# Attention and GRU in one kernel: the softmax's reciprocals through DRAM instead of TensorE, and another sequence of SyncE's transfers

## The chip, the cores and the metric

The kernel runs on one core of a Trainium2 chip. The metric is the device time in microseconds (us), the median of the runs shown. Engines: TensorE (PE, with its weight loads as PEld), VectorE (DVE), ScalarE (ACT), GpSimd (POOL), SyncE (SP), which here only issues DMA transfers, and the 16 DMA engines that carry them out.

## The reference, cut to what matters

`x` is 16 batches x 256 rows x 512, `cond` 16 x 512, all float32. An attention layer with 16 heads of 32 is followed by a GRU over the 256 rows.

```
xn = rms_norm(x, g_norm) * (1 + scale) + shift      # scale, shift = cond @ W_emb + b_emb
q, k, v = split(xn @ W_qkv); q, k = rms_norm(q, g_q), rms_norm(k, g_k)      # by head
attn = softmax(q k^T * 32 ** -0.5); o = attn v
x = x + o + o @ W_out
x = x + GRU(x, h0 = cond)                           # 256 steps, one after the other
```

## The kernel before

**Stages.** After a start of some 70 us comes the attention for the 16 batches, up to about 660 us, and then the 256 steps of the GRU up to the end, which the change leaves alone apart from how its weights `wih` are loaded.

**Passes.** The attention is done in 64 passes (`NP`), four for each batch b. Pass p = 4 b + w (w from 0 to 3) takes one half of the rows (i = 0 for w 0 and 1, i = 1 for w 2 and 3) and 8 of the 16 heads, in two units e = 0, 1 of four heads j. In a pass TensorE does: `scores` of the next pass (L612), `turn_p` of the two units, which transposes the exponentials P (L631), `turn_recips` (L654), two pieces of other work that the table `slots(p)` lists, and `times_v` (L646), which gives O for the pass with the dimension of a head on the partitions: partition 32 j + d, free (e, row). The pieces are mostly projections for the next batch n = b + 1 (`project`, 12 products, L552) and the output projection (`out_proj`, 12 products, L667). All projections and output projections use PSUM bank 6 in turn, so each waits until the one before was read out of it (`bank6_empty`). In w = 0 the pieces are `project(n, 0, 1)` and `project(n, 1, 1)`.

**Reciprocals.** The sums of the exponentials (`rsum`) stand with the row on the partition, but O needs their reciprocals with the row along the free dimension. So DVE takes the reciprocal at the end of pass p - 1 for pass p (`recips(p)`, L1041), spreads the 8 numbers of a row over 256 (`rB`, L1045), TensorE transposes them in pass p (L654) into bank 7, ACT copies them to `rTs` (`keep_recips`, L1305), and DVE multiplies O by them at the start of pass p + 1 (`scale(p)`, L947). In that same pass TensorE's `turn_p` waits for `scale` before its fifth transpose (semaphore `o`), since O and P transposed share a bank.

**The x of the next but one batch.** In w = 2 DVE turns the block-wise x of batch b + 1 out of the buffer `xb` (`turn_x`, L858, which counts `x_blocks_turned` up). SP may then load the x of the following batch into `xb` (`load_x`, L308): 16 DMAs of 32 KB, since each moves 32 partitions of one column block. In w = 0 ACT squares all of it (`square_blocks`, L1212, output `sqx`), which waits for all 16. It is the first thing that ACT does in a pass with w = 0; behind it stand, in this order, the copy of P transposed (`PT`, L1311), `keep_recips`, four exponentials with their sums (L1296), the copy of the projection out of bank 6 (`keep_raw`, L1251), its squares (L1270), `PT` again, four exponentials, `scale_q` (L1282), the second `keep_raw` and its squares. In w = 1 DVE sums these last squares and POOL raises them to the power -1/2 (`rsqrt`, L1486), then POOL scales `xb` for the next `turn_x`.

**Order.** All of it is written by hand: each engine runs its own list, and semaphores couple them. SP's list for a batch b is `load_x(b + 2)`, `store_q`, `load_q` (the q rows go through DRAM to be blocked), then the transfers of the output rows of batch b - 1 (`store_x1`, `load_residual`, `store_blocks`), `store_k`, `load_k`, and the output rows again. A wait of SP holds up all that stands behind it.

Of the kernel before, what the change touches and what calls it, by code (L numbers as in the profile page):

```python
# [5 lines left out]
F32 = mybir.dt.float32  # L6
# [6 lines left out]
NB = 16  # L13
T = 256
D = 512
# [13 lines left out]


# [20 lines left out]
for _p in range(NP):  # L51
    PASS += [("recips", _p)] + [_x for _slot in slots(_p) for _x in _slot if _x]
# [32 lines left out]
def cond_resid_kernel(nc, x, cond, W_emb, b_emb, g_norm, W_qkv, g_q, g_k, W_out, W_ih, W_hh, b_ih, b_hh, out):  # L85
    gscr = nc.dram_tensor("gscr", [NT, 128, 4, 3, 128], F32, kind="Internal").ap()
    xscr = nc.dram_tensor("xscr", [T, NB, D], F32, kind="Internal").ap()

# [5 lines left out]
    with ExitStack() as ctx:  # L94
# [30 lines left out]
        rinv = sb("rinv", [128, 8])  # L125
        rB = sb("rB", [128, 2, 128])
        rTs = sb("rTs", [128, 2, 256])
# [137 lines left out]
        s_wl = sem("wo_low_parts")  # L265
        s_gd = [sem("first_gates0"), sem("first_gates1")]
# [25 lines left out]
        def _(sp):  # L292
# [4 lines left out]
            def load_x(b):  # L297
# [7 lines left out]
                for a in range(4):  # L305
# [105 lines left out]
            for b in range(NB):  # L411
                if b + 2 < NB:
                    load_x(b + 2)
                if b:
                    store_q(b)
                    load_q(b)
                if b == NB - 1:

                    sp.wait_ge(s_qkv, 6 * b + 4)
                    for j in range(4):  # L420
                        for k in range(2):
                            load_whh(j, k)
# [4 lines left out]
                else:  # L427
                    load_residual(0, 0)
                    load_residual(0, 1)
# [15 lines left out]
                if 1 <= b <= 3:  # L445

                    g = b - 1
                    if g == 0:
                        sp.wait_ge(s_wsd, 3 * KC)
                        sp.wait_ge(s_ss, 1)  # L450
                    sp.dma_start(wih[:, :, g * D:(g + 1) * D],
                                 W_ih[:, g * D:(g + 1) * D].rearrange("(c p) n -> p c n", p=128)).then_inc(s_lwi, 16)
# [3 lines left out]
                if b:  # L456
                    store_blocks(b - 1, 1)
            store_x1(NB - 1, 0)
# [62 lines left out]
        def _(pe):  # L521
# [128 lines left out]
            def turn_recips(p):  # L650
                bank_free(("recips", p))
                pe.wait_ge(s_rb, p + 1)
# [99 lines left out]
            for p in range(NP):  # L752
# [3 lines left out]
                turn_recips(p)  # L756
# [18 lines left out]
            def gate_piece(tt, g, k):  # L775
# [3 lines left out]
                if k == 0:  # L779
# [6 lines left out]
                    else:  # L786
                        pe.wait_ge(s_lwi, 48)
# [40 lines left out]
        def _(v):  # L828
# [115 lines left out]
            def scale(p):  # L944
                emptied(v, ("recips", p))
                v.wait_ge(s_pv, p + 1)
                v.tensor_tensor(rTs[:, p % 2, :], pO, rTs[:, p % 2, :], ALU.mult).then_inc(s_o, 1)  # L947

            def high(p):
# [4 lines left out]
                if b and c == 0:  # L954
                    v.wait_ge(s_op, 2 * (b - 1) + i + 1)
                v.tensor_copy(oh[:, c:c + 2, 128 * i:128 * i + 128],
                              rTs[:, p % 2, :].rearrange("p (c t) -> p c t", c=2)).then_inc(s_oh, 1)
# [622 lines left out]
```

## Time and profile before

| | us |
|---|---|
| runs | 1695.72, 1695.76, 1696.96 |
| median | 1695.76 |
| the profiled execution | 1694.08 |
| its span | 1692.3 |
| PE busy in the span | 1661.7 |
| DVE, ACT, POOL busy | 1172.9, 962.1, 419.1 |
| from the first `load_x` of the steady part to the last | 70.67 to 549.20 |

The profiled execution has 1.8 us outside its span. TensorE is busy for 98% of the span at the full granted clock. The attention's steady part repeats with a period of four passes, one batch; the groups of rows below show one such period, mostly the one whose `load_x` starts at 350.04 us.

### The profile page before, as it was taken

To read this page: it belongs to the slowest core of one execution; us is meant where nothing else is said; L and a number is where in the kernel's file an instruction comes from. 1 tells how busy PE (TensorE), PEld (TensorE's weight loads), DVE (VectorE), ACT (ScalarE), POOL (GpSimd) and SP (SyncE) were. 2 spreads that over 40 slices of the span, in tenths; PEclk is the share of its full clock that TensorE was granted. 3 is DMA by queue.
4 is the path that set the end of the run, shared out by engine and by line. 5 is a ranking of instruction groups with operands and counts; after the bars stand their busy time and mean duration, and the time that the engine had idled before them with its cause. 6 is when DMAs were issued, how large, how long until landed. Compare 5 with 4: busy or idle time off the path is not lost.

```text
span 1692.3 us, 68244 instructions
## 1 busy us (share of the span) xinstructions
PE 1661.7 (98%) x28505; PEld 1221.0 (72%) x28505; DVE 1172.9 (69%) x4107; ACT 962.1 (57%) x3521; POOL 419.1 (25%) x478
## 2 busy tenths in 40 slices
PE   9999999999999998999999999999999999999996
PEld 6787788878887876666666666666766666667664
DVE  5888888888888876466666666666666666666665
ACT  5777777777777774344444444444444444444444
POOL 3544444444444432011111111111111111111111
PEclk9999999999999999999999999999999999999999
DMA  7244433334433336434433434434434334334331
GB/s 237 51 124 122 113 89 93 96 98 99 100 89 88 88 81 161 97 78 84 85 77 77 84 74 78 83 73 85 80 71 84 77 78 86 77 74 85 70 69 24
DMA packets 301963, 151.38 MB, mean 89 GB/s; under 512 B 142716, under 2 KB 281160, under 8 KB 301656
## 3 DMA queue, kind: packets, MB, share of 16 engines
q1 hardware_dynamic: 300272, 146.42, 39.2%
q8 instruction: 225, 3.69, 0.9%
q14 instruction: 82, 0.67, 0.1%
q10 hardware_dynamic: 1384, 0.60, 0.1%
HBM read 84.61 MB, written 62.13 MB: 87 GB/s over the span
## 4 chain that ended last, share of the span: by engine, by line
PE 93%; DVE 2%; ACT 1%; POOL 1%; DMA 1%; issue 1%; SPq 0%; POOLq 0%; DVEq 0%
PE ps L819 39%; PE ps L790 20%; PE ps L552 14%; PE ps L631 7%; PE ps L667 5%; PE ps L612 4%; PE ps L646 4%; PE ps L654 1%; DMA wstage<-in_L_cond_W_qkv_dram 1%; POOL rq L1486 1%; PE ps L591 0%; PE ps L573 0%; ACT P L1296 0%; DVE nmx L927 0%; DVE v L1144 0%
## 5 line engine op out<-in xcount | busy, mean ns | idle before, releaser
L819 PE MATMUL ps<-whh,hT 128*32 128x192 f32 x16384 | 713.1, 326 | 11.9 <-DVE hT L1170 11.9
L819 PEld LDWEIGHTS ps<-whh,hT 128*32 128x32 f32 x16384 | 496.0, 110 | 210.4 <-DVE hT L1170 81.7
L1421 ACT ACTIVATE v<-ps 128x128 f32<-128x128 f32 x512 | 139.2, 272 | 431.6 <-PE ps L819 431.6
L790 PE MATMUL ps<-wih,x1T 128*32 128x256 f32 x6144 | 376.6, 379 | 0.7 <-ACT x1T L1315 0.7
L1551 POOL TENSOR_TENSOR outG<-hG,GI 128x128 f32<-128x128 f32 x256 | 117.3, 458 | 905.7 <-DVE hG L1163 905.7
L1144 DVE SCALAR_TENSOR_TENSOR v<-v,ps 128x64 f32<-128x64 f32 x512 | 113.3, 221 | 275.0 <-ACT v L1421 275.0
L790 PEld LDWEIGHTS ps<-wih,x1T 128*32 128x32 f32 x6144 | 199.5, 110 | 106.7 <-ACT x1T L1315 0.9
L1296 ACT ACTIVATE P<-ps,nmx 128x256 f32<-128x256 f32 x496 | 229.6, 483 | 1.0 <-DVE nmx L927 1.0
L1429 ACT ACTIVATE v<-v 128x64 f32<-128x64 f32 x512 | 131.1, 256 | 106.6 <-DVE v L1149 106.5
L1486 POOL TENSOR_TENSOR rq<-msq,mh 128x16 f32<-128x16 f32 x64 | 185.9, 2905 | 5.3
L927 DVE TENSOR_REDUCE nmx<-ps 128x4 f32<-128x1024 f32 x128 | 155.9, 1218 | 18.3 <-PE ps L612 18.2
L1440 ACT COPY ps<-GI 128x192 f32<-128x192 f32 x510 | 162.6, 319 | 1.3 <-DMA GI<-gscr 1.3
L1159 DVE TENSOR_TENSOR v<-v,v 128x64 f32<-128x64 f32 x512 | 115.3, 225 | 64.0 <-ACT v L1429 48.7
L552 PE MATMUL ps<-wqh,xh 128*128 128x512 f32 x360 | 151.5, 421 | 0.1
L552 PE MATMUL ps<-wql,xh 128*128 128x512 f32 x360 | 141.6, 393 | 0.0
L552 PE MATMUL ps<-wqh,xl 128*128 128x512 f32 x360 | 140.5, 390 | 0.0
L631 PE MATMUL ps<-ident,P 128*128 128x128 f32 x1024 | 138.5, 277 | 1.7 <-DVE rTs L947 1.4
L631 PEld LDWEIGHTS ps<-ident,P 128*128 128x128 f32 x1024 | 114.3, 142 | 31.3 <-issue 20.8
L1425 ACT ACTIVATE v<-v 128x64 f32<-128x64 f32 x512 | 130.5, 255 | 8.1
L1170 DVE STREAM_TRANSPOSE hT<-hG 128x64 f32<-128x64 f32 x510 | 123.5, 242 | 8.8
L1311 ACT COPY PT<-ps 128x512 f32<-128x512 f32 x128 | 74.4, 581 | 95.1 <-PE ps L631 95.0
L1163 DVE SCALAR_TENSOR_TENSOR hG<-v,v 128x64 f32<-128x64 f32 x512 | 113.6, 222 | 8.8
(135 smaller groups left out, 1954.9 us busy)
## 6 DMA issues: line engine op xcount, KB each, us to landing
gscr<-nat SPq DMA_DIRECT2D x96, 256.0 KB, 2.9
GI<-gscr SPq DMA_DIRECT2D x124, 192.0 KB, 4.9
xres<-in_x_dram SPq DMA_DIRECT2D x32, 256.0 KB, 3.0
xscr<-x1s SPq DMA_DIRECT2D x32, 256.0 KB, 2.4
xblk<-x1s SPq DMA_DIRECT2D x128, 64.0 KB, 2.6
GI<-xscr SPq DMA_DIRECT2D x128, 64.0 KB, 2.5
out_dram<-outG SPq DMA_DIRECT2D x128, 64.0 KB, 2.2
x1n<-xblk SPq DMA_DIRECT2D x124, 64.0 KB, 2.5
```

The source lines that it names most:

```text
L552: last = pe.matmul(pB, xp[e2][:, c, m], wp[:, c, n], start=(k == 0), stop=(k == 3 * KC - 1))
L631: last = pe.transpose(pP[:, j, k, :], P[:, U % 4, j, 128 * k:128 * k + 128], ident)
L790: last = pe.matmul(F[G % 2][q, n], x1T[:, tt % 2, j, c, :], wih[:, c, g * D + 256 * half:g * D + 256 * half + 256], start=(c == 0), stop=( ...
L819: last = pe.matmul(ps[32 * j:32 * j + 32, q, 0:192], hT[:, 32 * c:32 * c + 32], whg[:, c, :, 128 * j + 64 * q:128 * j + 64 * q + 64], star ...
L927: done = v.tensor_reduce(nmx[:, p % 2, j, :], ps[:, j, :].rearrange("p j (e t) -> p j e t", e=2), AXX, ALU.max, negate=True)
L1170: v.transpose(hT[:, f[q]], h_new[:, f[q]]).then_inc(s_hc, 1)
L1296: last = s.activation(P[:, (2 * p + e) % 4, j, :], pS[e][:, j, :], ACT.Exp, scale=rq0[:, 4 * (2 * p + e) + j:4 * (2 * p + e) + j + 1] if p ...
L1421: s.activation(v_rz[:, q, :], ps[:, q, 64:192], ACT.Tanh, scale=0.5).then_inc(s_tr, 1)
L1425: s.activation(v_c[:, q, :], v_rz[:, q, 64:128], ACT.Copy, bias=0.5, scale=-0.5)
L1429: s.activation(v_n[:, q, :], v_w[:, q, :], ACT.Tanh).then_inc(s_n, 1)
L1440: s.copy(ps[:, q, 0:192].rearrange("p (g f) -> p g f", g=3), GI[(t + 1) // ST % 2][:, (t + 1) % ST, 0:3, 64 * q:64 * q + 64]).then_inc(s_s ...
L1486: g_.tensor_tensor(rq0 if k == 2 else rq[:, i, :], msq[:, i, :], mh, ALU.pow).then_inc(s_rq, 1)
```

## The change

For the passes p < 60 (`LATE`), the reciprocals no longer go over TensorE. DVE writes them into every eighth number of a 128 x 64 tile `rinv` (4 of 32 columns for each e; the rest was set to 1 once by POOL), transposes that in blocks of 32 x 32 into `rinvT`, SP stores it into a DRAM tensor `rscr` (one DMA, 32 KB), and loads it back four times 32 partitions wide, each row of numbers repeated on 32 partitions, into `rTs` (four DMAs). `rTs` is now laid out (g, e, t) with rows t in groups g of 32, so `scale`, `high` and `low` read it with another pattern. `turn_recips` and `keep_recips` are left only for the passes 60 to 63, the last batch.

SP's list gets five DMAs more for each of these passes, and is written in another sequence: `load_x` is split in two, one quarter ahead of `load_recips`, three quarters behind `store_q`. The weights `wih` are loaded in 12 DMAs of 256 KB, in the batches 1 to 12, instead of 3 of 1 MB in the batches 1 to 3.

```diff
+LATE = NP - 4
+            def store_recips(p):
+                sp.wait_ge(s_rt, p + 1)
+                if p >= 2:
+                    sp.wait_ge(s_rl[p % 2], 64 * (p // 2))
+                sp.dma_start(rscr[p % 2].rearrange("g j e t -> (g j) (e t)"), rinvT).then_inc(s_rs, 16)
+
+            def load_recips(p):
+
+                sp.wait_ge(s_rs, 16 * (p + 1))
+                if p >= 2:
+                    sp.wait_ge(s_ol, p - 1)
+                for j in range(4):
+                    sp.dma_start(rTs[32 * j:32 * j + 32, p % 2].rearrange("p g e t -> p g (e t)"),
+                                 rscr[p % 2, :, j].rearrange("g (o e) t -> o g (e t)", o=1).to_broadcast([32, 4, 64])).then_inc(s_rl[p % 2], 16)
...
-                if b + 2 < NB:
-                    load_x(b + 2)
-                if b:
+                if b == 0:
+                    load_x(2, 0, 1, 2, 3)
...
+                else:
+                    store_recips(4 * b - 1)
+                    if b + 2 < NB:
+                        load_x(b + 2, 0)
+                    load_recips(4 * b - 1)
                     store_q(b)
+                    if b + 2 < NB:
+                        load_x(b + 2, 1, 2, 3)
+                    if 4 * b < LATE:
+                        store_recips(4 * b)
                     load_q(b)
+                    if 4 * b < LATE:
+                        load_recips(4 * b)
...
                     store_blocks(b - 1, 0)
+                if b + 1 < NB:
+                    store_recips(4 * b + 1)
+                    load_recips(4 * b + 1)
...
                     load_k(b + 1)
+                    store_recips(4 * b + 2)
                 if b:
                     store_x1(b - 1, 1)
                     load_residual(b, 1)
                     store_blocks(b - 1, 1)
+                if b + 1 < NB:
+                    load_recips(4 * b + 2)
+                if 1 <= b <= 12:
...
+                    sp.dma_start(wih[:, c, g * D:(g + 1) * D], W_ih[128 * c:128 * c + 128, g * D:(g + 1) * D]).then_inc(s_lwi, 16)
...
                 turn_p(2 * p)
-                turn_recips(p)
+                if p >= LATE:
+                    turn_recips(p)
...
             def scale(p):
-                emptied(v, ("recips", p))
+                if p < LATE:
+                    v.wait_ge(s_rl[p % 2], 64 * (p // 2 + 1))
...
             def recips(p):
...
+                v.reciprocal(rinv[:, :, 0:4], rsum[:, p % 2, :, :]).then_inc(s_ri, 1)
                 v.wait_ge(s_ri, p + 1)
...
+                if p < LATE:
+                    if p:
+                        v.wait_ge(s_rs, 16 * p)
+                    v.transpose(rinvT, rinv.rearrange("p e j -> p (e j)")).then_inc(s_rt, 1)
+                    return
...
-                keep_recips(p)
+                if p >= LATE:
+                    keep_recips(p)
```

**SP, from the end of a pass with w = 2 on.** Before (L308 is `load_x`, L323 and L328 `store_q` and `load_q`, L338 `store_x1`; the waits are named by semaphore):

```order
L308 DMA xb<-in_x_dram 32x8x32 [waits x_blocks_turned]
L308 DMA xb<-in_x_dram 32x8x32 x15
L323 DMA qscr<-raw 128x512 [waits normed]
L328 DMA raw<-qscr 32x4x128 [waits q_out]
L328 DMA raw<-qscr 32x4x128 x3
L338 DMA xscr<-x1s_95 128x512 [waits bank6_empty]
```

Changed (L309 is `store_recips`, L317 `load_recips`, L331 `load_x`, L346 `store_q`, L351 `load_q`):

```order
L309 DMA rscr<-rinvT 128x64 [waits recips_in1,recips_by_blocks]
L331 DMA xb<-in_x_dram 32x8x32 [waits x_blocks_turned]
L331 DMA xb<-in_x_dram 32x8x32 x3
L317 DMA rTs<-rscr 32x4x64 [waits o_low,recips_out]
L317 DMA rTs<-rscr 32x4x64 x3
L346 DMA qscr<-raw 128x512 [waits normed]
L331 DMA xb<-in_x_dram 32x8x32 [waits x_blocks_turned]
L331 DMA xb<-in_x_dram 32x8x32 x11
L309 DMA rscr<-rinvT 128x64 [waits recips_in0,recips_by_blocks]
L351 DMA raw<-qscr 32x4x128 [waits q_out]
L351 DMA raw<-qscr 32x4x128 x3
```

The first DMA now waits for the reciprocals of the pass, six DMAs stand between the start of this stretch and the last DMA of `load_x` that did not before.

**DVE, at the end of the same pass.** Before:

```order
L858 STREAM_TRANSPOSE xt<-xb 128x1024 [waits k_blocks_turned,x_block_scaled]
L1041 RECIPROCAL rinv<-rsum 128x8 [waits exps]
L1045 COPY rB<-rinv 128x256 [waits recips,recips_turned]
L866 TENSOR_SCALAR xf<-xt,Aff,Shf 128x256 [waits x_low,x_blocks_turned]
L866 TENSOR_SCALAR xf<-xt,Aff,Shf 128x256
L947 TENSOR_TENSOR rTs<-ps,rTs 128x256 [waits pv,bank7_empty]
```

Changed:

```order
L897 STREAM_TRANSPOSE xt<-xb 128x1024 [waits k_blocks_turned,x_block_scaled]
L1088 RECIPROCAL rinv<-rsum 128x2x4 [waits recips_by_blocks,exps]
L1093 STREAM_TRANSPOSE rinvT<-rinv 128x64 [waits recips_out,recips]
L905 TENSOR_SCALAR xf<-xt,Aff,Shf 128x256 [waits x_low,x_blocks_turned]
L905 TENSOR_SCALAR xf<-xt,Aff,Shf 128x256
L990 TENSOR_TENSOR rTs<-ps,rTs 128x2x4x32 [waits pv,recips_in0]
```

The block transpose stands where the spreading copy stood, and `scale` waits for a DMA instead of bank 7.

## Rows read from the trace of the kernel before

**Rows 1.** The chain that ended last, 300 to 400 us, shares by line.

```profile
by line: PE ps L552 41.9%; PE ps L631 19.1%; PE ps L667 14.0%; PE ps L612 10.8%; PE ps L646 10.3%; PE ps L654 2.2%; PE ps L591 1.6%; PE ps L729 0.2%
```

**Rows 2.** That chain in order of time: start us, us, what.

```profile
362.84 0.22 PE ps L654 x2
...
370.52 1.08 PE ps L612 x16
```

**Rows 3.** Groups of instructions by line, whole span: busy us, mean ns, idle before.

```profile
L1170 DVE STREAM_TRANSPOSE hT<-hG 128x64 f32<-128x64 f32 x510 | 123.5, 242 | 8.8
L1045 DVE COPY rB<-rinv 128x256 f32<-128x256 f32 x64 | 31.3, 489 | 6.5
L654 PE MATMUL ps<-ident,rB 128*128 128x128 f32 x128 | 24.5, 273 | 0.0
L1305 ACT COPY rTs<-ps 128x256 f32<-128x256 f32 x64 | 23.9, 373 | 6.4 <-PE ps L654 2.2
```

**Rows 4.** Timeline of SP: start us, us spent issuing, line, transfer, count.

```profile
70.67 8.90 SPq L308 DMA_DIRECT2D xb<-in_x_dram  x16
...
350.04 9.18 SPq L308 DMA_DIRECT2D xb<-in_x_dram  x16
361.41 1.89 SPq L328 DMA_DIRECT2D raw<-qscr  x4
...
469.53 7.74 SPq L308 DMA_DIRECT2D xb<-in_x_dram  x16
...
549.20 7.75 SPq L308 DMA_DIRECT2D xb<-in_x_dram  x16
```

**Rows 5.** A DMA of load_x; queue q8, 353-354, 100-620 us; landing, 469-477; `kscr`.

```profile
353.11 1.66 SPq L308 DMA_DIRECT2D xb<-in_x_dram  x1
q8 instruction: 1, 0.02, 7.0%
q8 instruction: 38, 0.62, 0.5%
...
DMA to landing us min/median/max: 1.7/1.8/2.0
kscr<-xt SPq DMA_DIRECT2D x26, 256.0 KB, 2.0
```

**Rows 6.** Timeline of ACT and one row of PE, a pass with w = 0.

```profile
360.61 1.06 ACT L1212 ACTIVATE sqx<-xb 128x1024 f32<-128x1024 f32 x1 [1.12 <-DMA xb<-in_x_dram]
365.87 0.59 ACT L1251 COPY xt<-ps 128x512 f32<-128x512 f32 x1 [0.56 <-PE ps L552]
366.51 0.50 PE L552 MATMUL ps<-wqh,xh 128*128 128x512 f32 x1
367.02 0.57 ACT L1311 COPY PT<-ps 128x512 f32<-128x512 f32 x1
367.49 0.48 ACT L1296 ACTIVATE P<-ps,nmx 128x256 f32<-128x256 f32 x1
369.30 0.74 ACT L1282 ACTIVATE qT<-xt,gqs 128x512 f32<-128x512 f32 x1
370.75 0.63 ACT L1270 ACTIVATE sq<-xt 128x512 f32<-128x512 f32 x1
```

**Rows 7.** Timeline of ACT, DVE and POOL, from w = 1 to w = 3.

```profile
330.91 0.63 ACT L1270 ACTIVATE sq<-xt 128x512 f32<-128x512 f32 x1
...
341.12 2.90 POOL L1486 TENSOR_TENSOR rq<-msq,mh 128x16 f32<-128x16 f32 x1
344.05 0.69 DVE L882 TENSOR_TENSOR raw<-raw,rq 128x512 f32<-128x512 f32 x1 [0.49 <-POOL rq L1486]
...
348.78 1.23 DVE L858 STREAM_TRANSPOSE xt<-xb 128x1024 f32<-128x1024 f32 x1
349.93 0.16 DVE L1041 RECIPROCAL rinv<-rsum 128x8 f32<-128x8 f32 x1
...
353.82 0.68 DVE L882 TENSOR_TENSOR raw<-raw,rq 128x512 f32<-128x512 f32 x1
```

More of the change, by code:

```diff
@@ L51 @@
 for _p in range(NP):
-    PASS += [("recips", _p)] + [_x for _slot in slots(_p) for _x in _slot if _x]
+    PASS += ([("recips", _p)] if _p >= LATE else []) + [_x for _slot in slots(_p) for _x in _slot if _x]
 BANK = {p: 6 if p[0] in ("project", "out") else 7 for p in PASS}
@@ L295, in _, with load_x @@
             x_j = xscr.rearrange("(t s) b (j f) -> t j b s f", s=ST, j=4)
-            def load_x(b):
+            def store_recips(p):
[10 more added lines that the diff above has]
+                                 rscr[p % 2, :, j].rearrange("g (o e) t -> o g (e t)", o=1).to_broadcast([32, 4, 64])).then_inc(s_rl[p % 2], 16)
+            def load_x(b, *parts):
                 if b == 0:
@@ L304, in load_x @@
                     sp.wait_ge(s_xt, b - 2)
-                for a in range(4):
+                for a in parts:
                     for c in range(KC):
@@ L944, in scale @@
             def scale(p):
-                emptied(v, ("recips", p))
+                if p < LATE:
+                    v.wait_ge(s_rl[p % 2], 64 * (p // 2 + 1))
+                else:
+                    emptied(v, ("recips", p))
                 v.wait_ge(s_pv, p + 1)
-                v.tensor_tensor(rTs[:, p % 2, :], pO, rTs[:, p % 2, :], ALU.mult).then_inc(s_o, 1)
+                r = rTs[:, p % 2].rearrange("p g e t -> p e g t")
+                v.tensor_tensor(r, pO.rearrange("p (e g t) -> p e g t", e=2, g=4), r, ALU.mult).then_inc(s_o, 1)
             def high(p):
@@ L1301, in keep_recips @@
             def keep_recips(p):
-                s.wait_ge(s_rT, p + 1)
-                if p >= 2:
-                    s.wait_ge(s_ol, p - 1)
-                s.copy(rTs[:, p % 2, :], pR).then_inc(s_ev[7], 1)
+                s.wait_ge(s_rT, p - LATE + 1)
+                s.wait_ge(s_ol, p - 1)
+                s.copy(rTs[:, p % 2].rearrange("p g e t -> p e g t"), pR.rearrange("p (e g t) -> p e g t", e=2, g=4)).then_inc(s_ev[7], 1)
             def keep_turned_p(U):
@@ L1499, in _ @@
             g_.memset(mh, -0.5).then_inc(s_id, 1)
+            g_.memset(rinv, 1.0).then_inc(s_id, 1)
             rsqrt_x(0)
```

52 lines of the change are left out of this document (28 added, 24 removed).

## The prediction, made before the changed kernel was run

> **What bounds the kernel now.** I read the engines' busy shares first: TensorE is busy for 98% of the span, so a stage is paid for in TensorE's time unless something else is late. The chain of what ended last confirms it for the attention's steady part: from 300 to 400 us every link is TensorE's, no other engine and no DMA [rows 1]. The GRU behind it is untouched. So two questions decide: how much of TensorE's time goes, and which of the other engines' chains, now hidden, comes up when TensorE gets shorter and SP gets more to do. For the second I read SP's timeline, and then the timelines of ACT, DVE and POOL around the one DMA wait that ACT already has, 1.12 us before it squares the next x [rows 6].
>
> **What is removed.** The two transposes of reciprocals stand in the chain with 0.22 us a pass [rows 2], no more, although one lasts 273 ns by itself [rows 3]: they overlap. 60 passes give 60 x 0.22 = 13.2 us of TensorE. The period of four passes, 39.84 us, would become 39.84 - 4 x 0.22 = 38.96. ACT loses a copy of 373 ns a pass [rows 3], which it had room for. DVE swaps the spreading copy (489 ns mean) for a block transpose of 128 x 64 (242 ns for that shape, both [rows 3]): a little time off an engine with gaps, taken as nothing. The other patterns of `scale`, `high` and `low` keep runs of 32 numbers and the same count: nothing.
>
> **What is added to SP.** Per pass five DMAs. In a run without a disturbance 16 DMAs of `load_x` take 7.74 us, 0.49 each (the first 0.1 less) [rows 4]; the four of `load_q` took 1.89, and I take 0.45 each for the like-shaped ones of `load_recips`. So SP issues some 20 x 0.46 = 9 us more a period, on top of about 21. It has the time, but its list is in order, and the question is what stands behind these.
>
> **The load of x is what stands behind them.** Let T be the time at which `load_x` starts now (350.04 in the rows, when `turn_x` is done [rows 7]). Now the last of the 16 is issued at about T + 7.3 and lands 1.8 us later [rows 4, 5]; ACT needs all 16 for `sqx`. In the changed list:
> - SP waits for the turned reciprocals first. DVE starts the reciprocal at 349.93 [rows 7]; with 0.16, a hand-over of about 0.1 and the transpose of 0.24 they are there at T + 0.45.
> - One DMA for the store, 0.4, and a quarter of x, 4 x 0.49: T + 2.8. The store lands after 2.0 (as `kscr` [rows 5]), at T + 2.45, so `load_recips` need not wait: 4 x 0.45, T + 4.6.
> - `store_q`: its data is ready when DVE's L882 ends, 353.82 + 0.68, T + 4.46 [rows 7], so no wait: T + 5.1.
> - Three quarters of x: the last is issued at T + 5.1 + 11 x 0.49 = T + 10.5 and lands at T + 12.35.
>
> So `sqx` can start at T + 12.35 at the earliest, not at T + 9.1. That is too late for ACT's list in w = 0. Behind `sqx` come 1.0 us for itself, 0.47 for `PT` (367.02 to 367.49), 1.81 for four exponentials (367.49 to 369.30), so `keep_raw` starts 3.28 after `sqx` [rows 6]: T + 15.6. TensorE waits for that copy with its second projection: now it starts at 365.87, and the product begins at 366.51, just behind its end [rows 6]. T + 15.6 would be 365.67 in the times of the rows, which looks like no loss, but only until two things are put in: TensorE's own gain of three passes by then (0.66), and what disturbs SP.
>
> **The disturbance.** In 9 of the 13 periods `load_x` takes longer than 7.75 us, up to 9.3; the 13 rows (first 8.90, last 7.75) sum to 111.0, a mean of 8.54 [rows 4]. One DMA in it then needs 1.66 instead of 0.45 us, and in the same microsecond the instruction queue q8 moves one packet of 16 KB [rows 5]; such packets come 38 times in 520 us, every 13.7 [rows 5]. So a stretch of 8 us of issuing pays 0.8 us on average, 1.1 where it is hit (9 in 13). A stretch of 10.5 us should be hit 10.5 / 13.7 of the time: h = 0.77 x 1.1 = 0.85 us a period. I have only seen the coincidence, so for h the bounds are 0 and 1.43 (9.18 - 7.75 in each period); 0.85 is nearest to the rows.
> The Trainium skill ("Runtime: NRT & Kernel Launch", Instruction fetch mechanics) says that the sequencers fetch their next 16 KB block while executing the current one and that crossing a boundary is mostly hidden. By that rule h would be 0, and the sum below would come out as in the second rival; the rows of `load_x` so far speak against it.
>
> **The loop.** Late x makes a closed chain that has no gain in it. Let A be the end of ACT's last squares of w = 0.
> - A to T: 350.04 - (330.91 + 0.63) = 18.50 us [rows 7]. It is DVE's sum, POOL's powers and scaling of `xb`, its next power (until 344.02, for which DVE waits 0.49), and then DVE without a gap to `turn_x`. TensorE is not in it.
> - T to `sqx`: 12.35 + h.
> - `sqx` to the next A: 3.28, then from `keep_raw` to the end of the squares 370.75 + 0.63 - 365.87 = 5.51, without a gap on ACT [rows 6]: 8.79.
>
> Together 39.64 + h, with h = 0.85 a period of 40.49 us, against 39.88 now ((549.20 - 70.67) / 12 [rows 4]) and 38.96 for TensorE alone. The loop binds for every h from 0 up; TensorE gets its time back as a wait for bank 6 in w = 0 of (40.49 - 38.96) = 1.5 us.
>
> **The sum.** 12 periods x (40.49 - 39.88) = +7.3 us. In the last period with a load of x, `scores` of w = 1 starts at T + 13.2 + 3.28 + 0.64 (the copy and its hand-over) + 4.01 (366.51 to 370.52 [rows 2, 6]) = T + 21.1 instead of T + 20.5: +0.6. After it 7 passes gain 0.22 each: -1.5. The start and the GRU: 0; the smaller `wih` loads stand behind everything urgent: 0. Sum +6.4. On the profiled execution 1694.08 + 6.4 = 1700.5; the median of the runs is 1.7 above that execution, so **1702 us**, slower by 0.4%. An error of 0.25 us in T + 12.35 is 3 us in the sum, and 0.2 in h is 2.5, so this case reaches from 1697 to 1707.
>
> **Are the reciprocals themselves in time?** DVE turns them at the end of pass p - 1 and `scale(p)` needs them at the start of pass p + 1, some 10 us later. For the pass of the list above they land at about T + 6, and `scale` runs at T + 10.8. The tightest is the pass with w = 2, whose load stands behind six DMAs of output rows: about 6 us to issue, 2 to land, again two short of the 11. I take nothing, and keep a chance that one of them is late.
>
> **The rivals.**
> 1. The gain stays: TensorE's 13.2 us come off, 1695.8 - 13.2 = 1682.6. For it speaks that the chain is TensorE's alone [rows 1] and that the change gives `sqx` only some 3 us of delay, against room in ACT's list. It decides at about T + 11.7 for `sqx`: `keep_raw` at T + 15.0, in time for a product at 366.51 - 0.66. My count is 0.65 us later without, 1.5 us with the disturbance. It wins if SP issues its small DMAs faster, or x lands sooner, than I take.
> 2. The loop binds, but fetches cost SP nothing (h = 0): 12 x (39.64 - 39.88) = -2.9, the last period -0.3, the tail -1.5: -4.7, 1691. Against it speak the nine long rows of `load_x`.
> 3. The loop binds harder: a disturbance of 1.43 us in each period, 12 x (41.07 - 39.88) + 1.2 - 1.5 = +14, 1710. For it: more DMAs are open to it. Against: four periods of 13 had none.
> 4. Late reciprocals: `scale` waits for its DMA, and TensorE at its fifth transpose of P. Half a microsecond a period on top of the forecast would be 1708.
>
> **How the numbers follow.** A measurement of this kernel can tell about 0.2%, 3.4 us, from no change. Chances: forecast 0.62, rival 1 0.13, rival 2 0.10, rival 3 0.08, rival 4 0.07. Faster by over 0.2% (below 1692.4) are rival 1, most of rival 2 and a sliver of the forecast: 0.20. Within 0.2% (up to 1699.2) is the lower part of the forecast's range, 0.18, and the rest of rival 2: 0.22. Slower: 0.58. The range leaves out rival 1 and the upper end of rival 3: 1689 to 1709.
>
> **What the changed profile would show.** L654 with 8 instead of 128 instructions and TensorE's busy time some 13 us lower, with that much or more back as gaps; the wait of `sqx` for the load of x at 2 to 4 us a period instead of 1; TensorE waiting about 1.5 us for ACT's copy out of bank 6 in each pass with w = 0; the chain that ended last running through SP's `load_x`, ACT, DVE and POOL's L1486 line there; the period of `load_x` near 40.5 us, and 38.96 behind the last. Wrong would be a chain that is still TensorE's alone (rival 1), or waits of `scale` for DMA (rival 4), or a period near 39.6 (rival 2).

## The result: slower, by more than twice what was forecast

The changed kernel takes 1711.4 us (median of 4 runs, 1709.07 to 1711.66), the kernel before on the same chip 1695.99 (1695.72 to 1696.96): the ratio is 1.0086, 95% interval 1.0074 to 1.0098, or +14.6 us (+12.5 to +16.6). The forecast was 1702. The direction and the mechanism were right, the size was not, and the time lies above the range's upper end, 1709. The profiled execution took 1711.66 us, 1709.8 of it in the span: +17.5 us against the profiled one of before. Some 3 of these 17.5 us are TensorE's granted clock, which fell twice in this execution and not in the profiled one of before (both places are shown below).

**Where the time is.** The busy times by stretch, the steady part of before, then all of the change; the columns are the stretch, its length, and the busy us of PE, PEld, DVE, ACT and POOL, PE's granted clock, and the DMA share. The first stretch of the change ends with the first `load_x` of the steady part, the second with the last, the third with the GRU's first product.

```profile
70.67:549.20 478.53, 478.31 (x4400) 383.54 (x4396) 393.32 (x663) 360.64 (x1093) 221.63 (x145) 1.00 0.41 100
```

```profile
0.00:71.36 71.36, 64.83 (x467) 48.86 (x467) 50.02 (x91) 47.86 (x117) 35.10 (x40) 1.00 0.50 163
71.36:565.87 494.51, 473.66 (x4304) 373.60 (x4296) 383.81 (x664) 342.05 (x1044) 221.78 (x145) 1.00 0.47 113
565.87:686.04 120.17, 112.06 (x1086) 87.59 (x1078) 89.70 (x156) 79.85 (x254) 45.02 (x40) 0.99 0.52 122
686.04:1709.80 1023.76, 1005.17 (x22544) 701.78 (x22544) 638.68 (x3198) 469.55 (x2046) 117.28 (x256) 1.00 0.38 77
```

The loss is in the steady part, the second row of the change: 494.51 against 478.53, 16.0 us in 12 periods, 1.33 each. TensorE was idle there for 0.2 us before and is for 20.9 now. The rest is small: +0.7 (71.36 against 70.67), -0.1 and +1.0 (the same stretches of before are 120.30 and 1022.80 us long).

**What ends last there.** The chain from 300 to 400 us, where [rows 1] had TensorE alone:

```profile
by line: SPq L331 14.5%; issue 10.0%; DVE nmx L966 9.8%; POOL rq L1538 8.7%; ACT P L1348 7.3%; POOL xb L1521 5.7%; DMA xb<-in_x_dram 5.6%; POOL rxp L1518 4.9%; DVE ssq L914 4.1%; DVE xt L921 3.8%; SPq L317 3.8%; ACT xt L1303 2.8%; ACT PT L1
```

L331 is `load_x`, L317 `load_recips`, L1538 POOL's powers, L1521 its scaling of `xb`: the loop of the prediction. The waits from 100 to 620 us (us in total, times, longest) name its two ends, ACT's squares of x (L1264) behind the load, and TensorE behind the copy out of bank 6 (L1303):

```profile
ACT sqx L1264 <- DMA xb<-in_x_dram: 54.5, 12, 5.7
...
PEld ps L590 <- ACT xt L1303: 16.7, 12, 1.5
PE ps L590 <- ACT xt L1303: 13.8, 12, 1.2
DVE xt L940 <- DMA raw<-qscr: 12.8, 12, 2.3
```

**The loop, row by row.** One period, SP's timeline (start us, us spent issuing). The reciprocals are turned at 319.33 + 0.24 = 319.57 (DVE L1093), the first of the rows below; SP's follow.

```profile
319.33 0.24 DVE L1093 STREAM_TRANSPOSE rinvT<-rinv 128x64 f32<-128x64 f32 x1
```

```profile
319.61 0.34 SPq L309 DMA_DIRECT2D rscr<-rinvT  x1
320.00 1.91 SPq L331 DMA_DIRECT2D xb<-in_x_dram  x4
322.01 1.82 SPq L317 DMA_DIRECT2D rTs<-rscr  x4
323.87 0.43 SPq L346 DMA_DIRECT2D qscr<-raw  x1
324.34 5.89 SPq L331 DMA_DIRECT2D xb<-in_x_dram  x12
330.33 1.18 SPq L309 DMA_DIRECT2D rscr<-rinvT  x1
```

These answer to [rows 4]. All of it is issued nearly as counted: the last DMA of x starts at 329.78, 10.21 us after the turned reciprocals, where the prediction had 10.05. But it lands late (the chain's piece), and ACT's row behind it:

```profile
329.78 2.57 DMA xb<-in_x_dram
```

```profile
332.38 1.06 ACT L1264 ACTIVATE sqx<-xb 128x1024 f32<-128x1024 f32 x1 [3.97 <-DMA xb<-in_x_dram]
...
335.61 0.60 ACT L1303 COPY xt<-ps 128x512 f32<-128x512 f32 x1
336.25 0.63 ACT L1322 ACTIVATE sq<-xt 128x512 f32<-128x512 f32 x1
...
340.50 0.63 ACT L1322 ACTIVATE sq<-xt 128x512 f32<-128x512 f32 x1
```

From `sqx` to the end of ACT's last squares (A in the prediction) it is 340.50 + 0.63 - 332.38 = 8.75 us; from there to the next turned reciprocals 18.83 to 18.84 in all periods but one; and from those to `sqx` in the 13 periods 14.67, 13.43, 13.54, 13.19, 14.06, 12.95, 12.81, 14.52, 13.31, 13.03, 13.51, 13.19, 13.17 us, a mean of 13.49. The sum, 41.08, is the period (41.21) but for 0.13.

Nearly all of that 0.13 is one period, in which the clock fell. TensorE had been idle for 0.71 and 1.21 us just before, both times waiting for the late ACT, and then ran the second projection's products at 0.63 instead of 0.39 us. The stretch shows a granted clock of 0.64 (the number behind POOL's), and ACT's second copy waits for the products:

```profile
254.00:258.70 4.70, 4.63 (x16) 3.42 (x20) 2.26 (x4) 3.56 (x12) 3.10 (x2) 0.64 0.73 171
```

```profile
258.71 0.58 ACT L1303 COPY xt<-ps 128x512 f32<-128x512 f32 x1 [1.12 <-PE ps L590]
```

That period has 1.03 us more between `sqx` and A. From that A to the next turned reciprocals it is 0.25 more, since DVE's sum stood behind `scale`, which had waited for TensorE too.

### The profile page after: what moved, and what is told of

The parts are those of the page before. It is cut to its first block, busy times and chain, and to the rows that moved or that the text cites. A ratio compares the mean times of both kernels' runs of the same rounds, so it can differ in the third digit from the quotient of the medians.

```text
span 1709.8 us, 68312 instructions
## 1 busy us (share of the span) xinstructions
PE 1655.7 (97%) x28385; PEld 1211.8 (71%) x28385; DVE 1162.2 (68%) x4107; ACT 939.3 (55%) x3461; POOL 419.2 (25%) x479
## 4 chain that ended last, share of the span: by engine, by line
PE 63%; DVE 10%; SPq 8%; POOL 6%; ACT 6%; issue 4%; DMA 3%; POOLq 0%; DVEq 0%; ACTq 0%
PE ps L858 38%; PE ps L829 19%; SPq L331 6%; POOL rq L1538 3%; ACT P L1348 3%; DVE nmx L966 3%; DMA xb<-in_x_dram 2%; PE ps L590 2%; POOL xb L1521 1%; SPq L317 1%; POOL rxp L1518 1%; DVE ssq L914 1%; DVE xt L921 1%; PE ps L705 1%; ACT PT L1362 1%
## 5 line engine op out<-in xcount | busy, mean ns | idle before, releaser
L858 PE MATMUL ps<-whh,hT 128*32 128x192 f32 x16384 | 713.3, 326 | 11.9 <-DVE hT L1222 11.8
L1538 POOL TENSOR_TENSOR rq<-msq,mh 128x16 f32<-128x16 f32 x64 | 186.0, 2906 | 5.3
L1211 DVE TENSOR_TENSOR v<-v,v 128x64 f32<-128x64 f32 x512 | 115.4, 225 | 63.8 <-ACT v L1481 48.5
L1201 DVE SCALAR_TENSOR_TENSOR v<-v,GI 128x64 f32<-128x64 f32 x512 | 113.6, 222 | 8.8
```

Source lines behind the costliest of these rows:

```text
L858: last = pe.matmul(ps[32 * j:32 * j + 32, q, 0:192], hT[:, 32 * c:32 * c + 32], whg[:, c, :, 128 * j + 64 * q:128 * j + 64 * q + 64], star ...
L1538: g_.tensor_tensor(rq0 if k == 2 else rq[:, i, :], msq[:, i, :], mh, ALU.pow).then_inc(s_rq, 1)
```

## The experiments

Line numbers move a little from kernel to kernel. The kernel before was run beside each; its medians were 1694.26, 1694.19, 1696.08 and 1694.53 us on the four chips used here.

**1. TensorE's part taken away, SP's list as before.** The new DMAs are not issued, `load_x` stands whole and first again, and `scale` reads a constant tile, so the division by the sums is left out for the passes before 60.

```diff
+            def store_recips(p):
+                return
...
+            def load_recips(p):
+                return
```

> The changed kernel without the transport: no reciprocal goes to DRAM or back, O of the passes before 60 is multiplied by ones (the division by the softmax's sums is left out there), and SP's list is that of the kernel before. TensorE's two transposes and ACT's copy are gone as in the change. Theory L (the late load of x is the whole loss, and TensorE's two transposes are worth 0.22 us a pass): 60 x 0.22 = 13.2 us below before, about 1683, period of a batch 38.96 us, the chain that ended last all TensorE. Theory R (a shorter TensorE uncovers another engine's chain even with the old list, so part of the loss is not SP's): between 1690 and 1700, with waits of TensorE for ACT or DVE in each period.

Measured: 1689.3 us (6 runs), ratio 0.9968, interval 0.9955 to 0.998: 5.4 us faster, where 60 x 0.22 would be 13.2. So the gain of rival 1 was not to be had even with no transport at all. The chain from 300 to 400 us has POOL, DVE and ACT in it, with an unchanged load of x:

```profile
by line: PE ps L584 26.2%; PE ps L663 11.4%; POOL rq L1531 8.7%; PE ps L699 8.5%; PE ps L644 6.5%; PE ps L678 6.1%; DVE nmx L960 4.3%; POOL xb L1514 3.8%; ACT P L1341 3.7%; POOL rxp L1511 3.3%; issue 3.1%; DVE xt L915 2.6%; ACT xt L1296 2.4
```

Its pieces in order (start us, us) show the place: POOL scales `xb`, raises the sums of q to the power, DVE multiplies, TensorE turns q.

```profile
335.11 1.90 POOL xb L1514
...
337.38 2.91 POOL rq L1531
...
340.31 0.70 DVE raw L915
341.01 0.14 issue
341.15 0.63 PE ps L623 x4
```

This is a second loop. TensorE waits 0.3 us for it in each of 13 periods; it goes on over TensorE from the turn of q to the copy whose squares POOL needs next, so that only the passes that lie on TensorE's part of it gain. The period is 39.40 us (turn at 301.75, then 341.15), 0.44 less than 39.84, which fits two passes' transposes and not four.

**2. The second loop opened.** In w = 2 TensorE's turn of q is put one piece later, and ACT's copy of it too.

```diff
-        [(("project", n, 1, 0), ("turn", n, 0, 0), None), (("project", n, 0, 2), None, None)],
+        [(("project", n, 1, 0), None, None), (("project", n, 0, 2), ("turn", n, 0, 0), None)],
```

On experiment 1:

> The kernel no_transport (nothing goes through DRAM, the division is left out in the passes before 60) with TensorE's turn of the q rows of the first half moved from the ninth product of the first piece of w = 2 to the ninth of the second, 4 to 5 us later, and ACT's copy of it moved behind the second four exponentials. Theory S (the only thing that kept 5.0 instead of 13.2 us was the wait of that turn for DVE's product): the period falls from 39.40 to 38.96, another 5 us: 1682 to 1685. If another loop stands right behind it: no change, 1688 to 1690.

Measured: 1680.6 us (4 runs), ratio 0.9913, interval 0.9899 to 0.9928, that is 12.2 to 17.1 us faster; the 13.2 lies inside. The chain is TensorE's alone again:

```profile
by line: PE ps L584 44.1%; PE ps L663 20.0%; PE ps L699 14.0%; PE ps L644 10.8%; PE ps L678 10.1%; PE ps L623 1.3%; PE ps L761 0.2%
```

On the kernel before, as the control:

> The kernel before, with one edit: the turn of q in w = 2 stands one piece later in TensorE's list. It is the control for the kernel without any division, in which the same edit came with -15.5 us where 60 transposes' chain rows give 13.2. If TensorE's own work sets the period of the kernel before (39.84 us with a spare of 0.26 us at that turn), the edit has nothing to give: 1694 to 1697, and the 2.3 us above 13.2 are the transposes' or the copy's. If part of the 15.5 is the edit's own, this kernel is 2 to 3 us below the kernel before, 1692 to 1694.

Measured: 1694.72 us (10 runs), ratio 0.9996, interval 0.9987 to 1.0006. By itself the edit gives nothing, so the whole difference of the two kernels without division, some 9 us, is the second loop.

**3. SP's traffic added, TensorE's part kept.** The transposes, the copies and their use stay; SP's list is the changed one, and what it loads goes to a tile nobody reads.

```diff
-                    sp.dma_start(rTs[32 * j:32 * j + 32, p % 2].rearrange("p g e t -> p g (e t)"),
+                    sp.dma_start(rTd[32 * j:32 * j + 32, p % 2].rearrange("p g e t -> p g (e t)"),
```

> The changed kernel with TensorE's transposes, DVE's spreading copy and ACT's copy kept and used for every pass; the new DMAs run as in the change, in its order, but what they load lands in a tile that nobody reads. Theory L: the loop through SP's load of x sets the period whatever TensorE does, so the time is that of the change, 1711 (1708 to 1714), and the 13 us of transposes cost nothing. Theory R (the loss comes from scale's new wait, or from the new path of the data): about 1696 to 1700, since nobody waits for the new loads. If losses add up without a loop: 1711 + 13 = 1724.

Measured: 1717.15 us (4 runs), ratio 1.0135, interval 1.012 to 1.015. The traffic costs 22.9 us (20.3 to 25.4); the change, 14.6 (12.5 to 16.6). So the loss comes from the traffic, and dropping the transposes and their copies gives some 8 us of it back by these ratios, 5.6 by the spans of the two profiled executions (1715.4 and 1709.8). It was expected to give nothing (1708 to 1714). That is not TensorE's time, which is not the bound here: ACT's copy of the reciprocals lies inside the loop, between `sqx` and the copy out of bank 6.

```profile
335.17 1.06 ACT L1260 ACTIVATE sqx<-xb 128x1024 f32<-128x1024 f32 x1 [4.76 <-DMA xb<-in_x_dram]
...
336.60 0.38 ACT L1353 COPY rTs<-ps 128x256 f32<-128x256 f32 x1
...
343.57 0.63 ACT L1318 ACTIVATE sq<-xt 128x512 f32<-128x512 f32 x1
```

From `sqx` to A it is 9.03 us instead of 8.75, 3.6 us in 13 periods; the steady part is 498.20 us instead of 494.51, 3.7 longer. Behind it seven passes keep their transposes (7 x 0.22 = 1.5 us). Together that is 5.2 of the 5.6; what lies between 5.6 and 8, if anything, is not shown. Late reciprocals can't be the cause of the loss: this kernel doesn't use them.

**4. The whole of x first, reciprocals behind it.**

```diff
-                    store_recips(4 * b - 1)
                     if b + 2 < NB:
-                        load_x(b + 2, 0)
+                        load_x(b + 2, 0, 1, 2, 3)
+                    store_recips(4 * b - 1)
...
-                    if b + 2 < NB:
-                        load_x(b + 2, 1, 2, 3)
```

> The change with one edit in SP's list: all 16 DMAs of the load of x stand ahead of the store and the load of the reciprocals of the pass with w = 3. Theory L with the durations of the changed profile: the wait of ACT's sqx falls from 4.7 us to under 1.5 a period; the reciprocals are stored 7.8 us later and land about T + 14, 3 us after scale needs them, so TensorE waits for scale in w = 0 instead: keep_raw at T + 17.9 against T + 17.2 in the change, a period of about 41.7, 1714 to 1720. If the reciprocals' latency does not matter (a rival that puts the whole loss on the load of x): about 1683 to 1688.

Measured: 1742.82 us (4 runs), ratio 1.0286, interval 1.0271 to 1.0301. Now the reciprocals are late. TensorE waits for `scale` in a pass with w = 0 (L667 is its fifth transpose of P), and the projection behind the wait runs at 0.63 us a product, then at 0.39:

```profile
305.58 0.86 PE L667 MATMUL ps<-ident,P 128*128 128x128 f32 x4 [3.07 <-DVE rTs L988]
...
308.80 0.63 PE L588 MATMUL ps<-wqh,xh 128*128 128x512 f32 x1
...
309.50 0.39 PE L588 MATMUL ps<-wql,xh 128*128 128x512 f32 x1
```

The stretches show the clock (the number behind POOL's): 1.00 while the engine idles, 0.55 behind it, about the lower of its two levels (1.2 GHz of 2.4), and 0.98 after.

```profile
302.50:305.50 3.00, 0.01 (x1) 0.00 (x0) 0.40 (x2) 0.59 (x1) 0.00 (x0) 1.00 0.38 121
305.50:309.20 3.70, 3.62 (x11) 2.97 (x12) 3.67 (x7) 1.94 (x8) 0.00 (x0) 0.55 0.26 75
309.20:312.00 2.80, 2.80 (x17) 2.38 (x16) 1.04 (x2) 1.36 (x3) 0.00 (x0) 0.98 0.43 121
```

In 3.7 us at 0.55 TensorE did what takes about 2.0 at full clock. A stall of 3 us thus cost nearly 5, which my price for late reciprocals had left out. The clock falls like this ten times in the attention of this kernel, each time costing 1.7 us: 17 of the 23 us by which the time lies above the 1714 to 1720 that I expected. The sequence of the change is much better than this one.

**5. ACT's squares of x later.** The change, with `square_blocks` behind the first four exponentials of w = 0. If the late x is the cause, it should not matter any more.

```diff
-                if w == 0 and m < NB:
-                    square_blocks(m)
                 keep_turned_p(2 * p)
...
                     exps(p + 1, 0)
+                if w == 0 and m < NB:
+                    square_blocks(m)
```

> The whole change, with one edit on ACT: in the passes with w = 0 the squares of the next x (sqx) stand behind the first four exponentials instead of at the head of the pass. Theory L (late x holds up ACT's list): x lands some 13.5 us after the reciprocals are turned, ACT now asks for it only about 14 us after, so the wait shrinks from 4.7 to under 0.7 us a period and TensorE no longer waits for bank 6. What binds then is the second loop that the run without transport showed (TensorE's turn of q in w = 2 waits for POOL's power and DVE's product, period 39.40): 1689 to 1693, some 20 us below the change. Rival D (the additional DMAs cost in themselves, in landings and in SP's time): above 1700, with new waits of scale or turn_q in place of sqx's.

Measured: 1693.11 us (10 runs) against 1694.19, ratio 0.9994, interval 0.9985 to 1.0004. One moved line takes back all that the change lost: by the ratios 1.0086 - 0.9994, 15.6 us. It is not a gain of the move by itself: in a kernel whose x is in time the same move makes it slower (end of experiment 9). The wait of the squares, 54.5 us above, is gone, and what waits now is the second loop:

```profile
ACT sqx L1264 <- DMA xb<-in_x_dram: 0.5, 1, 0.5
```

```profile
DVE raw L921 <- POOL rq L1538: 10.8, 13, 1.4
...
PE ps L629 <- DVE raw L921: 6.1, 13, 1.0
```

With the turn of q later as well:

> The whole change with both edits: ACT's sqx behind the first four exponentials of w = 0, and the turn of q one piece later in w = 2. Theory L and S together: neither loop binds, TensorE's 13.2 us come off except where the load of q lands late: 1683 to 1689. If the load of x still binds through SP (reciprocals turned to x landed 13.5 us on average, 14.7 at most, and ACT asks for it some 14 us after): 1690 to 1694.

Measured: 1688.73 us (4 runs), ratio 0.9958, interval 0.9941 to 0.9975. That is some 6 us above what 13.2 us of gain would give: the period is 39.46 us and not 38.96. `load_x` still has 7.7% of the chain from 300 to 400 us, and DVE waits for the q rows, 21.2 us in 12 periods from 100 to 620, so transfers still stand on the path here.

**6. One DMA fewer ahead of the last x.** The change, with `store_q` behind the last three quarters of x.

```diff
-                    store_q(b)
                     if b + 2 < NB:
                         load_x(b + 2, 1, 2, 3)
+                    store_q(b)
```

> The change, with the store of the q rows moved from ahead of the last twelve DMAs of x to behind them. The last DMA of x is issued one short DMA earlier, 0.43 to 0.47 us. If the time from the turned reciprocals to the squares of x sets the period, the period falls by as much: 13 x 0.45 = 5.9 us, 1705.5. The q rows come back about 1 us later: DVE waits for them already now, 12.8 us in 12 periods, and if that wait is on the path too the gain is eaten up: 1711 or more. If something else than the last x sets the period, nothing changes: 1710 to 1713.

Measured: 1707.92 us (4 runs), ratio 1.0072, interval 1.0054 to 1.0089; beside the change's 1.0086 the intervals overlap, so the trace has to tell. In it the stretch from the turned reciprocals to `sqx` is 13.03 us on average, 0.46 less, the amount that was moved, and the period is 40.84 ((560.73 - 70.66) / 12 from turned to turned), 0.37 less. The missing 0.09 is at the other side of the loop: DVE waits longer for the q rows (12.8 us before), and three periods are 0.24 to 1.26 us longer between A and the turned reciprocals, 2.2 us together, against the 1.3 that the fallen clock costs in the change.

```profile
DVE xt L940 <- DMA raw<-qscr: 27.6, 12, 3.7
```

So the load of x does set the period, and what is taken from it comes off the period but for that wait.

**7. The instruction fetches shifted.** The change, with 32 tiny transposes more at the start, which moves TensorE's later instructions against the blocks in which they are fetched.

```diff
+            for _ in range(32):
+                pe.transpose(ps[0:16, 2, 0:16], ident[0:16, 0:16], ident[0:16, 0:16])
```

> The change with 32 small transposes more on TensorE in the start, which moves every later instruction of TensorE by a quarter of a 16 KB block. Nothing else differs. Theory F (a DMA issue of SP that takes 1.3 to 1.9 us instead of 0.45 is hit by a fetch of TensorE's instructions): the packets of q8 come some 3 us earlier relative to the load of x in the first periods, and the long issues with them; periods without a packet between the turned reciprocals and the landing of the last x have none. Theory G (the long issues come from the DMAs' own backlog): they stay at the same DMA of the list whatever q8 does. Time within 3 us of the change by either.

Measured: 1711.25 us, one run. Queue q8 moves a packet of 16 KB in each of the 13 stretches from the turned reciprocals to `sqx`, and two in some. In the change the stretches with two are the first and the eighth, 14.67 and 14.52 us, against 13.29 on average for the 11 others. With the shift they are the third and the tenth, 14.54 and 14.78 us, and the first has fallen to 13.47. SP's rows of that first period, of the change, then with the shift:

```profile
71.36 3.14 SPq L331 DMA_DIRECT2D xb<-in_x_dram  x4
```

```profile
71.34 1.91 SPq L331 DMA_DIRECT2D xb<-in_x_dram  x4
```

The packets of the first three stretches come 1.2 to 1.8 us earlier (3 were expected), and the long stretches move with them, so it is not the place in SP's list that is slow. One of them, the eighth with 14.45 us, is long with a single packet, and stays unexplained.

The other half of the test, a stretch without a packet, does not occur in these two kernels. It does in experiment 4: from the first DMA of x to `sqx` it is 9.21 and 9.15 us in the two stretches without any, and 9.83 to 11.04, 10.48 on average, in the ten with one inside: 1.3 us more (the thirteenth, with a packet on its very start, has 9.55).

**8. Another order for POOL.** POOL raises the sums of q to the power before it scales `xb`, to close the second loop sooner. Three kernels: the kernel before with it, the kernel of experiment 5, and that of experiment 9.

```diff
+                rsqrt(n, 0, 0)
                 if m < NB:
                     scale_blocks(m)
-                rsqrt(n, 0, 0)
```

> The kernel before with the same edit on POOL alone. Its chain is TensorE's alone in the steady part, so by theory S and L nothing changes: 1694 to 1696. If it gets faster by 2 us or more, the edit and not the shorter TensorE is what helps in the two kernels above.

> The kernel sqx_later with one more edit, on POOL: the power for q of the first half (rsqrt(n, 0, 0)) stands ahead of the scaling of the next x instead of behind it. Theory S (the second loop runs through POOL's order): the product that TensorE's turn waits for is ready some 2.6 us sooner, the period falls to TensorE's own 38.96 and the time to 1683 to 1688. If the second loop is not POOL's, no change against sqx_later.

> The kernel w3_near (three passes of four through DRAM, load of x as before) with the same edit on POOL. Theory S: its chain ran through POOL's L1562 in each period, so this gives the rest of the 45 x 0.22 = 9.9 us: 1684 to 1688, against 1693 without the edit. If the many DMAs hold it back instead: unchanged at 1693.

Measured: 1705.72, 1700.12 and 1702.61 us, ratios 1.0063 (1.0048 to 1.0078), 1.0033 (1.002 to 1.0046) and 1.0047 (1.0032 to 1.0062). It makes all three slower: the theory fell. In the kernel before with the edit, DVE's product with the powers now meets POOL's scaling (DVE, then POOL, then TensorE's wait):

```profile
306.78 2.15 DVE L882 TENSOR_TENSOR raw<-raw,rq 128x512 f32<-128x512 f32 x1
```

```profile
306.48 1.90 POOL L1469 TENSOR_TENSOR xb<-xb,rxp 128x1024 f32<-128x1024 f32 x1
```

```profile
309.08 0.63 PE L591 MATMUL ps<-ident,raw 128*128 128x128 f32 x4 [0.77 <-DVE raw L882]
```

The product takes 2.15 us instead of 0.69 [rows 7], and ends 0.55 us behind POOL's scaling. The Trainium skill ("SBUF — State Buffer", Who interferes with whom) says that a DVE instruction with two inputs in SBUF contends with a GpSimd instruction that reads SBUF, the ports that the two share being an exclusive lock. These rows agree in kind: the product starts 0.30 us behind POOL's scaling and ends behind it, though by less than the 0.69 us that it takes alone.

TensorE's wait for this product is 9.5 us in 13 periods here, where it is 0.5 in the kernel before; the loss is 10.7 us. In the other two kernels it rises from 6.8 to 14.0 and from 5.1 to 16.5 us, for losses of some 7 and 9 us.

**9. The critical pass over TensorE, the others over DRAM.** The passes with w = 3, whose five DMAs stand ahead of x, keep their transposes, and x is loaded whole and first.

```diff
+def far(p):
+    return p < LATE and p % 4 not in (3,)
...
-                        load_x(b + 2, 0)
+                        load_x(b + 2, 0, 1, 2, 3)
...
-                if p >= LATE:
+                if not far(p):
                     turn_recips(p)
```

> The change for three passes of four: the passes with w = 3 keep TensorE's transposes, and so SP's list at the load of x is that of the kernel before, with the store and load of w = 0 behind it. 45 passes lose the transposes. Theory L: no late x, 45 x 0.22 = 9.9 us below before, about 1686. A rival by which the many small DMAs cost by themselves (slower landings, more of SP's time), wherever they stand: 1693 to 1705, with waits of scale or turn_q for DMAs.

Measured: 1693.29 us (10 runs), ratio 0.999, interval 0.9981 to 0.9999. The second loop holds it (POOL L1562 has 8.7% of its chain). With the turn of q later as well:

> Three passes of four through DRAM, load of x as in the kernel before, the turn of q one piece later. Theory S: 45 x 0.22 = 9.9 us come off: 1684 to 1687, less a dip of the granted clock at the start of the GRU where it comes (it cost about 3 us in w3_near). If the small DMAs cost by themselves: 1692 to 1694 as without the edit.

Measured: **1684.8 us** (4 runs, 1683.19 to 1687.53), ratio 0.994, interval 0.9923 to 0.9956: faster than the kernel before by 10 us and the fastest that computes all. Its chain is TensorE's alone, though `sqx` still waits:

```profile
by line: PE ps L610 43.2%; PE ps L689 19.9%; PE ps L725 14.0%; PE ps L670 10.8%; PE ps L704 10.1%; PE ps L649 1.3%; PE ps L712 0.7%; PE ps L787 0.2%
```

```profile
ACT sqx L1287 <- DMA xb<-in_x_dram: 15.3, 12, 1.9
```

Of the 13.2 us, three passes in four should bring 9.9. And with the squares moved, too:

> The fastest version that keeps the whole computation (1684.8: the pass of the long list over TensorE, the turn of q one piece later), plus the squares of x moved behind the first four exponentials of w = 0. Its chain was TensorE's alone although the squares still waited 15.3 us in 12 periods for x. Theory: those waits are covered, so nothing is left to gain: 1684 to 1686. Rival: they reach TensorE in the hit periods, and the move gives 2 to 4 us more, 1681 to 1683. Against the move stands that the copy out of bank 6 is then ahead of the squares, but the first power of the next batch comes later: 1686 to 1690 if that is the next loop.

Measured: 1689.09 us (6 runs), ratio 0.9967, interval 0.9955 to 0.9979, slower than without. Where x is in time, the squares are better ahead: behind the exponentials they delay the copy out of bank 6 (L1326), and the chain has them in it.

```profile
319.68 1.23 DVE nmx L986
...
321.31 1.56 ACT P L1371 x7
322.87 0.58 ACT sqx L1287
...
323.69 0.60 ACT xt L1326
```

## Why the prediction was right about the direction and wrong about the size

| step | forecast | measured |
|---|---|---|
| A to the turned reciprocals | 18.50 + 0.45 = 18.95 | 18.84, and 0.25 more in one period (clock) |
| turned to `sqx`, undisturbed | 11.9 | 12.08 (10.21 issue, 1.87 landing) |
| disturbance h | 0.85 | 1.41 |
| `sqx` to A | 8.79 | 8.75, and 1.03 more in one period (clock) |
| period | 40.49 | 41.21 |
| 12 periods | +7.3 | +16.0 |
| last stretch and tail | -0.9 | -0.1 |
| start and GRU | 0 | +1.7 |

**The step that failed is h, in the paragraph on the disturbance.** 41.21 - 40.49 is 0.72 a period. h was 0.85 and measured 1.41: 0.56 of the 0.72. The rest is 0.03 of the undisturbed loop and 0.13 that is nearly all the fallen clock, a cost that the prediction put at nothing. Two things in h were mis-sized. I let a packet of q8 count only where it meets SP's 10.5 us of issuing. It also counts while the last x is landing: with one there, the last DMA lands after 2.57 to 3.00 us, otherwise after 1.83 to 2.31. The longest is in the period behind the one shown above:

```profile
371.48 3.00 DMA xb<-in_x_dram
```

The trace of before had a case too: in the period that starts at 429.69 the packet came 9.0 us after the first DMA, behind SP's issuing, and the last DMA landed after 2.21 us instead of about 1.8. I had counted that row, 7.96 us, as undisturbed.

And I took one packet per 13.7 us as a chance of 0.77 per stretch. The stretch that matters is 12 to 13.5 us long, and in this trace each of the 13 had at least one, 15 in all. 15 packets at (13.49 - 12.08) x 13 / 15 = 1.22 us each is what h comes to; the price of one was about right (1.1), the number was 1.15 instead of 0.77. In before 4 of 13 rows had none while SP issued because `load_x` was only 8 us long: I carried the rate over, but cut the window short. With the right window the rate gives 13.49 / 13.7 = 0.98 packets and h = 1.20; that there were 1.15 is where TensorE's packets happen to fall in this program, which a rate can't tell. My upper bound for h, 1.43, lies next to the 1.41 by luck: it was the excess of one long row, not a count of packets. Rival 3, with 0.08, was nearest (1710).

The Trainium skill ("Runtime: NRT & Kernel Launch", Instruction fetch mechanics) has the crossing from one block to the next mostly hidden behind execution. For the engine that fetches that may hold; for SP's small DMAs it doesn't here: experiment 7, a single run, moved the packets and the long stretches moved along. By which mechanism a packet of one queue delays the issuing of another is not shown.

**The undisturbed loop was right** to 0.03 us in the sum (39.64 against 39.67), in part by luck, since its three parts are off by -0.11, +0.18 and -0.04. Right, too, was the place where it would show: SP's `load_x`, ACT, DVE and POOL in the chain, and TensorE behind bank 6 (1.1 to 1.4 us a pass, forecast 1.5). Only the wait of `sqx` was said too small, 2 to 4 us; it is 4.5.

**"38.96 for TensorE alone" was wrong, without effect on the sum.** I subtracted four passes from TensorE's period and asked only for the load of x as the next bound. Experiment 1 shows another at 39.40, through POOL's power and the turn of q. Rival 1 (1682.6, 0.13) could not have come true: with no transport at all the kernel gains 5.4 us. I had priced one loop and called the other bound TensorE. It was there to be read. In the kernel before, DVE's product ends at 344.05 + 0.69 = 344.74 [rows 7] and the turn of q starts 0.15 us behind it:

```profile
344.89 0.63 PE L591 MATMUL ps<-ident,raw 128*128 128x128 f32 x4
```

That is the hand-over of 0.14 us that the same pair has in experiment 1, where TensorE is known to wait. So this input was already just in time, and the spare of 0.26 us that the expectation for the control speaks of was not there. The turn starts 0.29 us behind the product before it, 0.23 in the control, where its input is early: the second loop was already longer than TensorE's own work by 0.06 us, and TensorE's gain outside that loop could not show.

**TensorE's busy time** fell by 6.0 us, not 13. 120 transposes are gone, but products at the lower clock take longer, and with each new gap the overlap between neighbours is lost too. How much each of the two makes is not shown.

**Rival 4 is out:** in the change `scale` waits for TensorE and, by the profile, never for its DMA (row below, us, times, longest), and experiment 3 has the loss without the use of what is loaded. Experiment 4 shows what late reciprocals would cost.

```profile
DVE rTs L990 <- PE ps L684: 18.7, 38, 2.3
```

**The tail and the GRU.** Around the GRU's first products, at 686.04, the clock falls a second time in this trace:

```profile
684.00:688.20 4.20, 3.04 (x28) 1.52 (x32) 0.86 (x3) 0.58 (x1) 0.00 (x0) 0.59 0.55 106
```

4.20 us at 0.59 are 1.7 us lost, some 0.7 of it in the third stretch and 1.0 in the last. So the last stretch's +1.0 is the clock, and the third, -0.1, would be -0.8 without it: the forecast of -0.9 for the tail was right. The profiled execution of before shows 1.00 there, but the control of experiment 2, which is no faster or slower than before, shows 0.66 from 668 to 673 us. The fall comes and goes, and isn't the change's.

## What to carry to other kernels

When work goes from the bound engine to an engine or queue with room, the period is set by closed loops over several engines: list every loop that is within the hoped gain of the bound, not just the one that the change lengthens. Here one at 39.40 us held back 60% of the gain and another at 41.21 made a loss of it, and moving one step took each off the path. An input that arrives just one hand-over before its use is such a loop, even when the chain names only the bound engine. Where a short disturbance recurs, count it over the whole stretch from first issue to last landing; if that is as long as the distance between two of them, take one each time. And in a queue that is worked off in order, price every consumer: with the small DMAs ahead of x the kernel lost 14.6 us, with x ahead of them (experiment 4) it lost 48.5, since now theirs were late. What gained was to keep those of the one critical pass out of the queue (experiment 9).

## What the runs showed of the hardware

- A packet of 16 KB on the instruction queue costs a stream of small DMAs issued by SP about 1.2 us: one DMA takes up to 1.7 us to issue instead of 0.45, or the last one lands after 2.6 to 3.0 us instead of 1.9 (the change; experiments 4 and 7).
- After 3 us without work TensorE's granted clock was 0.55 for 3.7 us, so a stall costs more than its length. In the change it fell in one of 13 periods, to 0.64 over 4.7 us, after idle times of only 0.71 and 1.21 us.
- DVE's product of two SBUF operands took 2.15 us instead of 0.69 next to POOL's scaling in SBUF. In the kernel before, DVE's spreading copy (L1045) shows the like: at 339.73, beside that scaling, it took 1.17 us, as 14 of the 64 took 1.0 us or more and 49 took 0.29.
